# Three self-attention stages of a Perceiver kernel on one core: values spread by way of device memory, jobs in another order, cosines on GpSimd

## The chip, the core and the metric

One of the eight cores of a Trainium2 chip runs the whole program. The time is the device time of one execution in microseconds (us). The engines are TensorE (PE, with its weight loads as PEld), VectorE (DVE), ScalarE (ACT), GpSimd (POOL) and SyncE (SP), which here only issues DMAs. They run side by side and meet at semaphores; each takes its own instructions in order.

## The reference

A state x of 32 sequences with 32 tokens and 256 channels goes through twelve stages, each of which adds its result to x. Three of them are self-attentions with 16 heads of 16 channels over the 32 tokens of a sequence:

```python
# l0a: rotary q and k, a decay by distance for softmax, a gate
Q = _rotary(proj(Wq, bq)); K = _rotary(proj(Wk, bk)); V = proj(Wv, bv)
out = einsum('bhts,bhsd->bhtd', (Q @ K.T) / sqrt(16) * exp(-sigmoid(gamma) * clip(t - s, 0)), V)
x = x + silu(n @ Wg.T + bg) * out
# l1a: rotary, q and k divided by their norm, softmax, output weights
x = x + softmax(q @ k.T / sqrt(16)) @ v @ Wo + bo
# l3f: q divided by its norm, moved and scaled; softmax; 17 gate columns pick heads
h = softmax((q / norm(q) + e) * softplus(T) @ k.T / sqrt(16)) @ v
x = x + (h * gates(h)) @ Wp.T + bp
```

Here n is x after a layernorm without weights. All numbers are float32.

## The kernel before, in words

`self_attention` builds each of the three stages; `build` calls it as l0a, l1a and l3f. The 1024 tokens are cut into NG = 8 tiles of P = 128 rows, GB = 4 sequences of LQ = 32 tokens each. A tile g goes through jobs, for each of which TensorE fills one of two PSUM banks in turn, so that a job waits until the job two before it has been evacuated:

- `n` (line 1069): the normalised rows, made by VectorE, are transposed; ScalarE copies them to `nT` (1334).
- `qk` (1075): queries and keys from `nT`; ScalarE evacuates them to `qk` (1339, or four instructions with a bias, 1343).
- `v` (1078): values; VectorE (1198, with a bias row) or ScalarE (1347) evacuates them to `V_own`.
- `rot` (1084, l0a and l1a): a matrix that swaps the pairs; VectorE multiplies by the sine into `tmp` (1203), multiplies `qk` by the cosine (1204) and adds (1206).
- `gate` (1081, l0a): the gate; VectorE adds a bias (1230), ScalarE applies Silu (1403).
- `norm` (1087, l1a and l3f): VectorE squares into `tmp` (1212), TensorE sums within heads, ScalarE makes the reciprocal root by a logarithm (1351) and an exponential (1353) into `rstd`, and VectorE scales (1217 to 1220).

VectorE then spreads the queries over two masked heads (`two_heads`, 1224), and TensorE computes scores (1098). With softmax, VectorE takes the row maxima (1182) and subtracts them (1183), ScalarE exponentiates (1360), VectorE sums, divides and transposes to `pT` (1187 to 1192). In l0a VectorE multiplies by the decay (1175) and transposes (1180). TensorE multiplies by the values (1113). For this it needs each sequence's values on each of four groups of 32 partitions: SP copies them from `V_own` into `V` by 16 DMAs of 32 x 256 a tile (1317), each counted on a semaphore. In l1a and l3f ScalarE copies the heads (1366), TensorE transposes them (1120), ScalarE copies that (1374), and TensorE multiplies by the output weights (1126; in l3f also by 17 gate columns, 1129). VectorE adds the result to x (1246). In l3f ScalarE keeps it first (1379), and VectorE weighs four tiles at once, after tiles 3 and 7 (`gate_heads`, 1247 to 1274).

The order of all this is written out by hand, as one loop on each engine with a software pipeline: in step `it` TensorE projects tile `it`, takes scores of tile `it - 1` and weighted values and output of tile `it - 2`. An instruction waits behind all that stand ahead of it on its engine, needed or not. GpSimd only raises the variances to the power -1/2 (`power`, 188 and 193).

## Time and profile before

| | us |
|---|---|
| median of 3 runs | 4350.17 (4343.62 to 4352.81) |
| the profiled execution | 4349.88 |
| its span | 4348.1 |
| TensorE busy in the span | 3857.8 (89%) |
| VectorE busy | 2601.9 (60%) |
| ScalarE busy | 1840.4 (42%) |
| GpSimd busy | 309.6 (7%) |

The shares are means over twelve stages with different limits, so they do not tell what bounds the three stages here; the views by stretch and by time do. A row of the timeline gives the start, the length, the engine, the line, the operation, what it writes and reads, the shape and the count. In brackets stands how long the engine was idle before it, and what ended that.

### The profile page before, as it was taken

To read this page: it belongs to the slowest core of one execution; us is meant where nothing else is said; L and a number is where in the kernel's file an instruction comes from. 1 tells how busy PE (TensorE), PEld (TensorE's weight loads), DVE (VectorE), ACT (ScalarE), POOL (GpSimd) and SP (SyncE) were. 2 spreads that over 40 slices of the span, in tenths; PEclk is the share of its full clock that TensorE was granted. 3 is DMA by queue.
4 is the path that set the end of the run, shared out by engine and by line. 5 is a ranking of instruction groups with operands and counts; after the bars stand their busy time and mean duration, and the time that the engine had idled before them with its cause. 6 is when DMAs were issued, how large, how long until landed. Compare 5 with 4: busy or idle time off the path is not lost. (4 is left out here: it accounts for less than half of the span.)

```text
span 4348.1 us, 100504 instructions
## 1 busy us (share of the span) xinstructions
PE 3857.8 (89%) x41564; PEld 2896.4 (67%) x41564; DVE 2601.9 (60%) x5431; ACT 1840.4 (42%) x5087; POOL 309.6 (7%) x560
## 2 busy tenths in 40 slices
PE   7986995999999999999999998659678879888866
PEld 6765984677777777777777776548545569555535
DVE  3435113777777777777777775641157757446635
ACT  2221321444555455455445444212166736346522
POOL 0000101000000000000000000020111100000000
PEclk9997997999999999999999999969899979999977
DMA  4111484001101101101111100127654410000001
GB/s 155 61 63 41 150 298 166 31 31 53 50 31 53 50 31 53 50 31 53 50 33 50 50 31 11 48 83 288 215 166 147 154 47 1 26 30 30 11 2 49
DMA packets 135347, 323.03 MB, mean 74 GB/s; under 512 B 35496, under 2 KB 94056, under 8 KB 110448
## 3 DMA queue, kind: packets, MB, share of 16 engines
q1 hardware_dynamic: 131824, 308.22, 21.2%
q0 software_dynamic: 3072, 8.39, 0.5%
q8 instruction: 333, 5.46, 0.5%
q14 instruction: 118, 0.97, 0.1%
HBM read 289.01 MB, written 14.94 MB: 70 GB/s over the span
## 5 line engine op out<-in xcount | busy, mean ns | idle before, releaser
L2580 ACT COPY layers_pT<-banks 128x512 f32<-128x512 f32 x384 | 227.7, 593 | 551.3 <-PE banks L2348 550.6
L2272 PE MATMUL banks<-ctx_tiles,weights_a 128*128 128x512 f32 x768 | 363.7, 596 | 0.0
L2279 PE MATMUL banks<-weights_a,ctx_tiles 128*128 128x256 f32 x1536 | 363.1, 379 | 0.0
L2573 ACT ACTIVATE layers_probs<-banks,layers_negmax 128x256 f32<-128x256 f32 x768 | 354.9, 481 | 13.7 <-DVE layers_negmax L2438 6.8
L2279 PEld LDWEIGHTS banks<-weights_a,ctx_tiles 128*128 128x128 f32 x1536 | 284.7, 190 | 76.1 <-issue 46.4
L2416 DVE TENSOR_TENSOR layers_V<-banks,rows_a 128x512 f32<-128x512 f32 x192 | 132.8, 692 | 220.5 <-PE banks L2279 216.6
L2348 PE MATMUL banks<-const,layers_probs 128*128 128x128 f32 x1536 | 244.0, 281 | 2.8 <-ACT layers_pT L2580 2.8
L2348 PEld LDWEIGHTS banks<-const,layers_probs 128*128 128x128 f32 x1536 | 171.1, 141 | 106.2 <-issue 96.2
L2437 DVE TENSOR_REDUCE layers_negmax<-banks 128x4 f32<-128x1024 f32 x192 | 233.8, 1218 | 3.0 <-PE banks L2340 2.8
L2540 ACT ACTIVATE layers_KT<-banks,layers_less_last 128x256 f32<-128x256 f32 x384 | 162.4, 481 | 157.5 <-PE banks L2272 157.5
L2340 PE MATMUL banks<-layers_KT,layers_qblk 32*64 32x256 f32 x3072 | 210.6, 388 | 0.0
L2272 PEld LDWEIGHTS banks<-ctx_tiles,weights_a 128*128 128x128 f32 x768 | 132.0, 192 | 93.2 <-issue 93.2
L2323 PE MATMUL banks<-layers_dm_nT,weights_b 128*128 128x128 f32 x1536 | 189.7, 277 | 0.6 <-ACT layers_dm_nT L2535 0.6
L2323 PEld LDWEIGHTS banks<-layers_dm_nT,weights_b 128*128 128x128 f32 x1536 | 181.6, 194 | 0.9 <-ACT layers_dm_nT L2535 0.9
L2328 PE MATMUL banks<-weights_b,layers_hid 128*128 128x256 f32 x768 | 176.9, 383 | 4.2 <-ACT layers_hid L2563 3.1
L2328 PEld LDWEIGHTS banks<-weights_b,layers_hid 128*128 128x128 f32 x768 | 142.4, 190 | 37.3 <-issue 18.6
L2573 ACT ACTIVATION_READ_ACCUMULATOR layers_probs<-banks,layers_negmax 128x1 f32 x768 | 162.7, 212 | 0.0
L2340 PEld LDWEIGHTS banks<-layers_KT,layers_qblk 32*64 32x64 f32 x3072 | 98.2, 131 | 73.4 <-issue 40.3
L2563 ACT ACTIVATE layers_hid<-banks,layers_dm_cols 128x128 f32<-128x128 f32 x384 | 111.1, 383 | 62.0 <-PE banks L2323 61.9
L2360 PE MATMUL banks<-layers_pT,layers_V 128*32 128x64 f32 x6144 | 125.5, 221 | 6.0 <-ACT layers_pT L2580 6.0
L2861 PE MATMUL banks<-weights_a,ctx_tiles 128*128 128x512 f32 x256 | 129.8, 636 | 1.0 <-DVE l2x_own L2936 0.5
L2360 PEld LDWEIGHTS banks<-layers_pT,layers_V 128*32 128x32 f32 x6144 | 96.2, 110 | 46.7 <-issue 40.0
(715 smaller groups left out, 8188.4 us busy)
## 6 DMA issues: line engine op xcount, KB each, us to landing
ctx_tiles<-in_ctx SPq DMA_DIRECT2D x65, 1028.0 KB, 5.1
weights_a<-in_L_w SPq DMA_DIRECT2D x44, 1024.0 KB, 5.3
l2x_B<-positions SPq DMA_DIRECT2D x32, 1280.0 KB, 5.9
weights_b<-in_L_w SPq DMA_DIRECT2D x32, 1024.0 KB, 5.2
weights_c<-in_L_w SPq DMA_DIRECT2D x16, 1024.0 KB, 7.2
weights_b<-in_L_xattn_w SPq DMA_DIRECT2D x12, 1024.0 KB, 7.4
l0x_key_rows<-in_ctx_rows SPq DMA_DIRECT2D x32, 256.0 KB, 2.7
ctx_tiles<-in_ctx_keys SPq DMA_DIRECT2D x32, 256.0 KB, 2.8
```

The costliest lines, as they stand in the source:

```text
L2272: last = mm(o.rearrange("p (j k) -> p j k", j=2), ca_wk[:, c, m * P:(m + 1) * P], keys, start=c == 0, stop=c == DC - 1)
L2279: last = mm(o[:, b * D:(b + 1) * D], E.ctx[:, tile % 2, c, first:first + P], ca_wv[:, c], start=c == 0, stop=c == DC - 1)
L2323: last = mm(o[:, i * P:(i + 1) * P], dm_w1[:, c, m * P:(m + 1) * P], dm_nT[:, c], start=c == 0, stop=c == DC - 1)
L2328: last = mm(o[:, 0:D], hid[:, m], dm_w2[:, m], start=m == 0, stop=m == FC - 1)
L2340: last = mm(ps[half, r // 2, a * KW:(a + 1) * KW], qblk[rows, tile % 2, cc, j + a], KT[rows, tile % 2, cc, (j + a) * KW:(j + a + 1) * KW], ...
L2348: last = tr(ps[:, TURN, (KC * t + c) * P:(KC * t + c + 1) * P], probs[:, cc, j, t, c * P:(c + 1) * P], E.c("ident"))
L2360: last = mm(ps[32 * i:32 * (i + 1), PV, j * 64:(j + 1) * 64], V[:, pos % 2, KC * j + c, cc * P + 32 * i:cc * P + 32 * (i + 1)], pT[:, k % ...
L2416: last = v.tensor_tensor(V[:, tile % 2, KC * arg:KC * (arg + 1)], o.rearrange("p (b d) -> p b d", b=KC), E.rA[:, 0].unsqueeze(1).to_broadc ...
L2437: link(v.tensor_reduce(peak, ps[:, 0:2].rearrange("p t (a x) -> p t a x", a=2), AX.X, ALU.max, negate=True))
L2540: last = a(KT[:, pos % 2, m, j * KW:(j + 1) * KW], o[:, j % 2 * KW:(j % 2 + 1) * KW], ACT.Identity, bias=less_last[:, pos // NG % 2, m, se ...
L2573: a(probs[:, cc, i, t], ps[:, t, i % 2 * KW:(i % 2 + 1) * KW], ACT.Exp, bias=negmax[:, cc, t, i:i + 1], accum_out=totals[:, cc, t, i:i + 1 ...
L2580: nc.scalar.copy(pT[:, k % 4].rearrange("p t c x -> p (t c x)"), ps[:, TURN]).then_inc(s["copied"], 1)
```

## The change

Four things, all in `self_attention`:

1. SP stores a tile's `V_own` to device memory (`value_rows`) with one DMA, waits until it has landed, and loads it into `V` by four DMAs, one for each group of 32 partitions. `V_own` is free again when the store has landed.
2. The loops of TensorE, VectorE and ScalarE are written in another order, and `n` stands second in the list of jobs.
3. With rotation, GpSimd multiplies `qk` by the cosine into a tile of its own, `turned_qk`, and VectorE only adds.
4. In l1a VectorE scales the keys alone, and scales and masks the queries in the same two instructions.

```diff
                  "rot": "dve", "gate": "dve", "norm": "act"}
-    kinds = ["qk", "v"] + (["rot"] if rope else []) + (["gate"] if gated else []) + ["n"] + (["norm"] if norms else [])
+    kinds = ["qk", "n", "v"] + (["rot"] if rope else []) + (["gate"] if gated else []) + (["norm"] if norms else [])
     jobs = [("n", 0)]
...
         s, handles = signals(st, nc, tag, "n_ready job_done evac_dve evac_act rotated squared logs rstd_ready qblk_ready scores_done shifted exp_done pT_ready "
-                             "pv_done attn_ready turned attnT_ready y_ready y_taken gate_in gate_ready scored gate_exp v_spread0 v_spread1 dve_step var_ready added_eps power_ready")
+                             "pv_done attn_ready cosine_ready turned attnT_ready y_ready y_taken gate_in gate_ready scored gate_exp v_stored v_spread0 v_spread1 dve_step var_ready added_eps power_ready")
 
...
         tmp, rstd = sb("tmp", [4 * P]), sb("rstd", [4 * P])
+        turned_qk = sb("turned_qk", [4 * P]) if rope else None
         V_own = sb("V_own", [2, D])
...
         def wait_spread(eng, tile):
-            eng.wait_ge(s[f"v_spread{tile % 2}"], 16 * GB * 4 * (tile // 2 + 1))
+            eng.wait_ge(s[f"v_spread{tile % 2}"], 16 * 4 * (tile // 2 + 1))
 
...
                         job("qk", it)
-                    if tile_in(it - 1):
-                        scores(it - 1)
+                    if tile_in(it + 1):
+                        job("n", it + 1)
                     if tile_in(it):
...
                             job("rot", it)
+                    if tile_in(it - 1):
+                        scores(it - 1)
                     if tile_in(it - 2):
...
                         job("gate", it)
+                    if tile_in(it) and norms:
+                        job("norm", it)
                     if tile_in(it - 2) and not gated:
                         turned(it - 2)
-                    if tile_in(it + 1):
-                        job("n", it + 1)
-                    if tile_in(it) and norms:
-                        job("norm", it)
                     if tile_in(it - 2) and not gated:
...
                     if g >= 2:
-                        wait_spread(dve, g - 2)
+                        dve.wait_ge(s["v_stored"], 16 * (g - 1))
                     v.tensor_tensor(V_own[:, g % 2], bank(number["v", g])[:, 0:D], bv_row, ALU.add).then_inc(s["evac_dve"], 1)
...
                     wait_job(dve, "rot", g)
-                    q4, t4 = qk[:, g % 2].rearrange("p a (j q) -> p (a j) q", j=GB), tmp.rearrange("p (a q) -> p a q", q=LQ)
+                    q4 = qk[:, g % 2].rearrange("p a b -> p (a b)")
+                    t4 = tmp.rearrange("p (a q) -> p a q", q=LQ)
                     v.tensor_tensor(t4, bank(number["rot", g]).rearrange("p (a q) -> p a q", q=LQ), E.c("sin").unsqueeze(1).to_broadcast([P, 16, LQ]), ALU.mult).then_inc(s["evac_dve"], 1)
-                    link(v.tensor_tensor(q4, q4, E.c("cos").unsqueeze(1).to_broadcast([P, 16, LQ]), ALU.mult))
                     wait_evacuated(dve, "rot", g)
-                    link(v.tensor_tensor(q4, q4, t4, ALU.add))
+                    dve.wait_ge(s["cosine_ready"], g + 1)
+                    v.tensor_tensor(q4, turned_qk[:], tmp[:], ALU.add).then_inc(s["rotated"], 1)
+                    dve.wait_ge(s["rotated"], g + 1)
 
...
                     dve.wait_ge(s["rstd_ready"], g + 1)
+                    if unit_norm:
+                        own = qk[:, g % 2, 2:4].rearrange("p a b -> p (a b)")
+                        v.tensor_tensor(own, own, rstd[:, 2 * P:4 * P], ALU.mult)
+                        for h in range(2):
+                            last = v.scalar_tensor_tensor(qblk[:, g % 2].rearrange("p m j (h q) -> p m j h q", h=2)[:, :, :, h],
+                                                          qk[:, g % 2, 0:2].rearrange("p m (j q) -> p m j q", j=GB), E.c("qmask32")[:, h:h + 1],
+                                                          rstd[:, 0:2 * P].rearrange("p (m j q) -> p m j q", m=DC, j=GB), ALU.mult, ALU.mult)
+                        last.then_inc(s["qblk_ready"], 1)
+                        return
                     link(v.tensor_tensor(q2, q2, rstd[:, 0:norm_cols], ALU.mult))
...
                 for it in range(NG + 3):
-                    if tile_in(it - 1):
-                        shift(it - 1)
                     if tile_in(it - 3) and not gated and heads_gate is None:
...
                         square(it)
+                    if tile_in(it - 1):
+                        shift(it - 1)
                     if tile_in(it) and gated:
...
                             scale(it)
-                        two_heads(it)
+                        if not unit_norm:
+                            two_heads(it)
 
...
                     wait_evacuated(sp, "v", g)
+                    sp.dma_start(E.value_rows[g], V_own[:, g % 2]).then_inc(s["v_stored"], 16)
+                    sp.wait_ge(s["v_stored"], 16 * (g + 1))
                     if g >= 3:
                         sp.wait_ge(s["pv_done"], g - 2)
-                    for j in range(GB):
-                        for b in range(4):
-                            sp.dma_start(V[LQ * b:LQ * (b + 1), g % 3, j], V_own[LQ * j:LQ * (j + 1), g % 2]).then_inc(s[f"v_spread{g % 2}"], 16)
+                    for b in range(4):
+                        sp.dma_start(V[LQ * b:LQ * (b + 1), g % 3], E.value_rows[g].rearrange("(j p) d -> p j d", j=GB)).then_inc(s[f"v_spread{g % 2}"], 16)
 
...
             def _(pool):
-                for g in range(NG):
-                    power(E, pool, s, g, stats[:, g, 8:9], stats[:, g, 7:8], 1e-5)
+                for g in range(NG + 3):
+                    if rope and g >= 3:
+                        wait_evacuated(pool, "qk", g - 3)
+                        if g >= 4:
+                            pool.wait_ge(s["rotated"], g - 3)
+                        nc.gpsimd.tensor_tensor(turned_qk.rearrange("p (a q) -> p a q", q=LQ), qk[:, (g - 3) % 2].rearrange("p a (j q) -> p (a j) q", j=GB),
+                                                E.c("cos").unsqueeze(1).to_broadcast([P, 16, LQ]), ALU.mult).then_inc(s["cosine_ready"], 1)
+                    if g < NG:
+                        power(E, pool, s, g, stats[:, g, 8:9], stats[:, g, 7:8], 1e-5)
 
...
                         if g >= 2:
-                            wait_spread(act, g - 2)
+                            act.wait_ge(s["v_stored"], 16 * (g - 1))
                         last = nc.scalar.copy(V_own[:, g % 2], o[:, 0:D])
...
                         keep_output(it - 3)
+                    if heads_gate is not None and it - 3 in (GB - 1, NG - 1):
+                        exponentiate_odds((it - 3) // GB)
+                    if tile_in(it + 1):
+                        take("n", it + 1)
+                    if tile_in(it):
+                        take("v", it)
                     if tile_in(it - 1) and decay is None:
                         exponentials(it - 1)
-                    if heads_gate is not None and it - 3 in (GB - 1, NG - 1):
-                        exponentiate_odds((it - 3) // GB)
-                    if tile_in(it):
-                        take("v", it)
                     if tile_in(it - 2) and not gated:
...
                         a(gate[:, it % 3], gate[:, it % 3], ACT.Silu).then_inc(s["gate_ready"], 1)
+                    if tile_in(it) and norms:
+                        take("norm", it)
                     if tile_in(it - 2) and not gated:
                         turned(it - 2)
-                    if tile_in(it + 1):
-                        take("n", it + 1)
-                    if tile_in(it) and norms:
-                        take("norm", it)
 
...
         E.sorted_out = nc.dram_tensor("sorted_out", (NBLK, P, D), F32).ap()
+        E.value_rows = nc.dram_tensor("value_rows", (NG, P, D), F32).ap()
         E.positions = nc.dram_tensor("positions", (2, NG, GB, 16 * NK * LQ), F32).ap()
```

What order this gives in the middle of l1a. `l1a_qk` are rotated queries and keys, `weights_a` and `rows_a` weights and bias rows, `const` holds tables and small matrices, `banks` is PSUM. Line numbers grow by up to 21 with the change.

TensorE, one tile, before:

```order
L1075 MATMUL banks<-l1a_nT,weights_a 128x128 x8
L1098 MATMUL banks<-l1a_qk,l1a_qblk 64x32 x32
L1078 MATMUL banks<-weights_a,l1a_nT 128x256 x2
L1084 MATMUL banks<-l1a_qk,const 128x512
L1113 MATMUL banks<-l1a_V,l1a_pT 32x16 x64
L1120 MATMUL banks<-const,l1a_attn 128x128 x2
L1069 MATMUL banks<-const,l1a_n 128x128 x2
L1087 MATMUL banks<-l1a_tmp,const 128x512
L1126 MATMUL banks<-weights_a,l1a_attnT 128x256 x2
```
and with the change:

```order
L1076 MATMUL banks<-l1a_nT,weights_a 128x128 x8
L1070 MATMUL banks<-const,l1a_n 128x128 x2
L1079 MATMUL banks<-weights_a,l1a_nT 128x256 x2
L1085 MATMUL banks<-l1a_qk,const 128x512
L1099 MATMUL banks<-l1a_qk,l1a_qblk 64x32 x32
L1114 MATMUL banks<-l1a_V,l1a_pT 32x16 x64
L1088 MATMUL banks<-l1a_tmp,const 128x512
L1121 MATMUL banks<-const,l1a_attn 128x128 x2
L1127 MATMUL banks<-weights_a,l1a_attnT 128x256 x2
```

The scores of the tile before (64x32) moved from second place to behind the rotation, the transposes of the next tile (`l1a_n`) from behind the turned heads to second place, the norm (`l1a_tmp`) ahead of them.

ScalarE, one tile, before:

```order
L1339 COPY l1a_qk<-banks 128x512
L1360 ACTIVATE l1a_probs<-l1a_probs 128x512
L1347 COPY l1a_V_own<-banks 128x256
L1366 COPY l1a_attn<-banks 128x4x4x16
L1374 COPY l1a_attnT<-banks 128x128 x2
L1334 COPY l1a_nT<-banks 128x256
L1351 ACTIVATE l1a_rstd<-banks,const 128x512
L1353 ACTIVATE l1a_rstd<-l1a_rstd 128x512
```
and with the change:

```order
L1360 COPY l1a_qk<-banks 128x512
L1355 COPY l1a_nT<-banks 128x256
L1368 COPY l1a_V_own<-banks 128x256
L1381 ACTIVATE l1a_probs<-l1a_probs 128x512
L1387 COPY l1a_attn<-banks 128x4x4x16
L1372 ACTIVATE l1a_rstd<-banks,const 128x512
L1374 ACTIVATE l1a_rstd<-l1a_rstd 128x512
L1395 COPY l1a_attnT<-banks 128x128 x2
```

The exponentials (`l1a_probs`) moved behind the two evacuations, the norm (`l1a_rstd`) ahead of the copy of the turned heads (`l1a_attnT`), which is last now.

VectorE, from the row maxima to the sum of the exponentials, before:

```order
L1182 TENSOR_REDUCE l1a_max<-banks 128x16
L1183 TENSOR_TENSOR l1a_probs<-banks,l1a_max 128x512
L1244 TENSOR_TENSOR l1a_attn<-banks,rows_a 128x256
L1246 TENSOR_TENSOR x_state<-x_state,l1a_attn 128x256
L1203 TENSOR_TENSOR l1a_tmp<-banks,const 128x512
L1204 TENSOR_TENSOR l1a_qk<-l1a_qk,const 128x512
L1206 TENSOR_TENSOR l1a_qk<-l1a_qk,l1a_tmp 128x512
L1212 TENSOR_TENSOR l1a_tmp<-l1a_qk 128x512
L1187 TENSOR_REDUCE l1a_sum<-l1a_probs 128x16
```
and with the change, from the stage's result:

```order
L1256 TENSOR_TENSOR l1a_attn<-banks,rows_a 128x256
L1258 TENSOR_TENSOR x_state<-x_state,l1a_attn 128x256
L1205 TENSOR_TENSOR l1a_tmp<-banks,const 128x512
L1208 TENSOR_TENSOR l1a_qk<-l1a_turned_qk,l1a_tmp 128x512
L1215 TENSOR_TENSOR l1a_tmp<-l1a_qk 128x512
L1183 TENSOR_REDUCE l1a_max<-banks 128x16
L1184 TENSOR_TENSOR l1a_probs<-banks,l1a_max 128x512
L1188 TENSOR_REDUCE l1a_sum<-l1a_probs 128x16
```

The maxima and the subtraction moved from ahead of the result, rotation and squares to behind them, and the multiplication of `l1a_qk` by the cosine (from `const`) is gone.

## Rows read from the trace of the kernel before

**Rows 1.** Busy time by stretch, l0a, l1a, l3f: us, PE, PEld, DVE, ACT, POOL, PEclk, DMA, GB/s.
```profile
318.00:422.00 104.00, 70.59 (x1760) 56.42 (x1760) 52.76 (x120) 15.96 (x49) 6.88 (x16) 0.80 0.19 51
2729.00:2838.00 109.00, 79.20 (x1792) 58.83 (x1792) 74.65 (x144) 32.81 (x73) 8.31 (x16) 0.88 0.19 49
4225.00:4342.00 117.00, 82.84 (x1808) 70.38 (x1808) 68.17 (x174) 37.71 (x107) 6.66 (x16) 0.72 0.16 38
```

**Rows 2.** Timeline of SP's DMA queue, l0a.
```profile
326.95 90.59 SPq L1317 DMA_DIRECT2D l0a_V<-l0a_V_own  x128
```

**Rows 3.** Busy time in one tile of l0a at full clock.
```profile
371.88:380.67 8.79, 7.62 (x220) 6.18 (x221) 6.50 (x16) 1.82 (x6) 0.90 (x2) 1.00 0.21 51
```

**Rows 4.** Timeline of TensorE, l0a: first and last projections, last weighted values.
```profile
321.90 3.69 PE L1075 MATMUL banks<-l0a_nT,weights_c 128*128 128x128 f32 x16 [0.46 <-ACT l0a_nT L1334]
...
389.65 2.02 PE L1075 MATMUL banks<-l0a_nT,weights_c 128*128 128x128 f32 x16 [1.17 <-ACT l0a_nT L1334]
...
418.92 1.57 PE L1113 MATMUL banks<-l0a_V,l0a_pT 32*32 32x16 f32 x128 [9.10 <-DMA l0a_V<-l0a_V_own]
```

**Rows 5.** Timeline of VectorE, the last sum of l0a.
```profile
421.41 0.42 DVE L1239 TENSOR_TENSOR x_state<-x_state,l0a_attn 128x256 f32<-128x256 f32 x1
```

**Rows 6.** Timeline of TensorE, l1a.
```profile
2732.32 3.40 PE L1075 MATMUL banks<-l1a_nT,weights_a 128*128 128x128 f32 x16 [0.46 <-ACT l1a_nT L1334]
...
2775.22 1.95 PE L1075 MATMUL banks<-l1a_nT,weights_a 128*128 128x128 f32 x16
...
2779.93 1.02 PE L1084 MATMUL banks<-l1a_qk,const 128*128 128x512 f32 x2
...
2785.17 1.03 PE L1126 MATMUL banks<-weights_a,l1a_attnT 128*128 128x256 f32 x4
...
2786.03 1.95 PE L1075 MATMUL banks<-l1a_nT,weights_a 128*128 128x128 f32 x16
...
2810.53 1.95 PE L1075 MATMUL banks<-l1a_nT,weights_a 128*128 128x128 f32 x16
```

**Rows 7.** Timeline of VectorE, l1a, in the same tile.
```profile
2779.11 0.69 DVE L1182 TENSOR_REDUCE l1a_max<-banks 128x16 f32<-128x512 f32 x1 [1.26 <-PE banks L1098]
...
2779.83 0.69 DVE L1183 TENSOR_TENSOR l1a_probs<-banks,l1a_max 128x512 f32<-128x512 f32 x1
...
2781.95 0.68 DVE L1204 TENSOR_TENSOR l1a_qk<-l1a_qk,const 128x512 f32<-128x512 f32 x1
```

**Rows 8.** Timeline of ScalarE, l1a, in the same tile.
```profile
2777.21 0.59 ACT L1339 COPY l1a_qk<-banks 128x512 f32<-128x512 f32 x1 [1.30 <-PE banks L1075]
...
2780.56 0.63 ACT L1360 ACTIVATE l1a_probs<-l1a_probs 128x512 f32<-128x512 f32 x1 [2.77 <-DVE l1a_probs L1183]
...
2782.47 0.37 ACT L1366 COPY l1a_attn<-banks 128x256 f32<-128x256 f32 x1 [1.02 <-PE banks L1113]
...
2783.37 0.43 ACT L1374 COPY l1a_attnT<-banks 128x128 f32<-128x128 f32 x2 [0.53 <-PE banks L1120]
...
2785.37 0.69 ACT L1351 ACTIVATE l1a_rstd<-banks,const 128x512 f32<-128x512 f32 x1 [1.29 <-PE banks L1087]
...
2786.09 0.63 ACT L1353 ACTIVATE l1a_rstd<-l1a_rstd 128x512 f32<-128x512 f32 x1
```

**Rows 9.** Timeline of TensorE, l3f: first and last projections.
```profile
4228.55 3.79 PE L1075 MATMUL banks<-l3f_nT,weights_c 128*128 128x128 f32 x16 [0.46 <-ACT l3f_nT L1334]
...
4306.06 3.30 PE L1075 MATMUL banks<-l3f_nT,weights_c 128*128 128x128 f32 x16
```

**Rows 10.** Timeline of ScalarE, l3f: evacuation of the projections with a bias.
```profile
4278.48 1.14 ACT L1343 ACTIVATE l3f_qk<-banks,cols 128x128 f32<-128x128 f32 x4 [2.37 <-PE banks L1075]
```

**Rows 11.** Busy time in l3f's last gating of the heads.
```profile
4333.60:4341.90 8.30, 0.00 (x0) 0.00 (x0) 7.04 (x27) 0.32 (x2) 0.00 (x0) 0.50 0.00 0
```

**Rows 12.** DMA issues of the page: a store to device memory (KB each, us to landing).
```profile
sorted_out<-l0f_y SPq DMA_DIRECT2D x23, 128.0 KB, 2.7
```

**Rows 13.** GpSimd by line: ns of one (least/median/most), first and last start, forms.
```profile
L3035 POOL TENSOR_TENSOR ctx_tiles<-ctx_tiles x32: 1037/1044/2292, 3142.8 to 3446.7; 128x512 f32<-128x512 f32 x32
```

## The prediction

> **What bounds the kernel now.** The change touches three stages of the program, the self-attentions l0a, l1a and l3f, so I read the stretches first: they last 104, 109 and 117 us of a span of 4348.1 us, with a mean granted clock of 0.80, 0.88 and 0.72 [rows 1]. Everything outside them keeps its instructions and its time. Then the DMA queue's timeline: in l0a SP issues 128 copies in 90.59 us without a pause worth the name [rows 2], 16 a tile, so SP needs about 10 us for a tile's values. Then TensorE's timeline. In l0a an undisturbed tile has 7.62 us of TensorE work in a pitch of 8.79 us at full clock [rows 3], less than SP's 10: SP falls behind, and at the end the stage waits for it. The last tile's projections (line 1075) start at 389.65, but its probability-times-values product (line 1113) only at 418.92, after 9.10 us of waiting for the DMA into V [rows 4], and the stage's last sum starts at 421.41 [rows 5].
>
> l1a is bound elsewhere. A tile there takes 10.81 us from projections to projections [rows 6]; VectorE stands still only 1.26 us in that, before the row maxima, waiting for the scores [rows 7]. So VectorE is the bound, and SP's 10 us hide. l3f is mixed: 77.5 us for seven tiles (4228.55 to 4306.06 [rows 9]), one of which carries the gating of the heads, 8.3 us [rows 11].
>
> **The change, part by part.** *Spread of values.* Sixteen copies a tile become one store to device memory, a wait, and four loads. SP issued a copy every 0.7 us (90.59/128 [rows 2]). A 128 KB store to device memory lands in 2.7 us [rows 12]; I take that for the store and for each load too. So V is ready 0.6 + 2.7 + 4 x 0.6 + 2.7 = 8.4 us after its values are evacuated; SP is busy 6 us of that, less than any tile's pitch. Bounds: about 5 us if transfers land at once, 13 if they take twice as long. The values are used two tiles later, so only the last tile could show it.
>
> *l0a.* The new order on TensorE is projections, next tile's transposes, values, rotation, scores, weighted values, gate. ScalarE's evacuation of the projections, formerly covered by the scores, now stands open before the values job: 0.9 us of waiting, where before TensorE waited about 1.2 us for the evacuated transposes. The pitch stays about 8.7 (7.62 + 0.9 and hand-overs). Tile 0 has neither scores nor weighted values and tile 1 only scores: 7.9 and 7.3. Seven tiles: 7.9 + 7.3 + 5 x 8.7 = 58.7, and a slow patch of 1, against 67.8 (321.90 to 389.65 [rows 4]): 8 us gained. The tail: masked queries ready 10.8 us after the last projections start, scores 1.1, decay and transposition 1.5, weighted values 1.6, two sums 0.9, hand-overs and a slow clock 1.6: 17.5, against 32.2 (389.65 to 421.83 [rows 4, 5]): 14 us gained. V, evacuated 4.9 us after those projections start, is ready at 13.3; it is needed at 14. Together **-22 us** for l0a; the upper bound of the round trip gives back 4.
>
> *The cosine on GpSimd.* It takes 0.68 us off VectorE a tile [rows 7] and costs GpSimd 1.04 us alone, 2.29 at worst for the same shape [rows 13]. It starts when ScalarE has evacuated the projections and is wanted after rotation and sine, some 2.7 us later in l1a. So it is hidden at either price, and counts as nothing; without that cover it would cost the difference, under 0.5 us a tile.
>
> *l1a.* Here the order makes a loop out of nearly everything. The exponentials of the tile before stand behind the row maxima, which VectorE now takes only after sine, sum and squares of this tile; ScalarE's copy of the heads, its logarithm and exponential for the norm and its copy of the turned heads stand behind those exponentials; and TensorE's output product, last in its tile, waits for that copy. In start-to-start steps: projections to evacuation 1.99 [rows 6, 8], evacuation 0.65 with the hand-over [rows 8], values 0.86 (as long as the output job, of the same form), rotation 1.06 [rows 6], five VectorE steps, four of 0.72 and one of 0.69 with 0.04 of hand-over [rows 7], ScalarE 0.63 + 0.37 + 0.69 + 0.63 + 0.43 = 2.75 [rows 8], output 0.92 with its hand-over. Sum **11.8 us**, against 10.81: VectorE has less to do and waits more. The rewritten scaling (three instructions on 256 columns in place of three) lies in that wait: nothing. First tiles: tile 0, without a predecessor, 9.3; tile 1, without output, 7.9; tile 2, whose VectorE is still late from tile 1, 12.5; then 4 x 11.8. Sum 76.9, against 78.2 (2732.32 to 2810.53 [rows 6]). That 78.2 holds its slow patches; 76.9 holds none.
>
> *l3f.* The same loop without rotation, sine, sum and squares (-3.2), with scores in their place (+1.1), four biased evacuations of 1.14 in all [rows 10] for 0.59, a norm of half the columns, a biased copy and 17 gate columns: 10.5 us a tile. First tiles 6.6, 5.9, 13.0, then 3 x 10.5, and the tile with the gating 18: 75, against 77.5.
>
> *Slow clock.* Projections take 1.95 us at full clock and up to 3.79 at the lower of TensorE's two levels, 1.2 GHz for 2.4 [rows 6, 9]: 1.8 us for each patch that falls on them. Nothing before shows how often the new order meets one. Bounds: never, and always. Mean clocks of 0.88 and 0.72 [rows 1] say neither; I take four patches in each of the two stages, 7.2 us, since the loop leaves TensorE more waiting than VectorE's chain did. So l1a +6, l3f +5. Tails of both: the same links, nothing.
>
> **Sum.** 4349.9 (the profiled execution, 1.8 us more than its span, 0.3 under the median of the runs) - 22 + 6 + 5 = **4339 us**.
>
> A rule bears on that clock. The stage with the lowest clock, l3f, had TensorE busy 71% of its stretch, l0a with 0.80 had it busy 68% [rows 1]: busy share alone does not order them. The Trainium skill, "TensorE: Matmul & The Clock Gate", Part 1, says that the throttled state is the default and that activity releases it. Taken alone, the rule would turn every longer wait into slow clock and add up to the 44 us of rival C; these rows make it only likelier, so the sum keeps four patches.
>
> **The rivals.** *B, a patch in every tile:* seven a stage, 12.6 us each instead of 7.2: 4349, no change. For: the loop repeats the same pauses in each tile. Against: the tile of l1a in [rows 6] has pauses too, and its projections take 1.95, which is full clock.
>
> *C, slower:* in l1a and l3f TensorE drops to 1.2 GHz and stays there, because a slower loop waits longer still. The price for a tile is what the loop holds of TensorE: projections 1.84, values, rotation and output some 0.9 each in l1a: 4.6; in l3f 4.3. Over five tiles each, 44 us on the sum without patches (-26): 4368. The gain is gone once six in ten of those tiles are slow, and eight in ten make the kernel slower by more than a measurement can miss. For: 0.72 in l3f now. Against: 0.88 in l1a.
>
> *D, no patches:* -22 - 1.3 - 2.5: 4324.
>
> *E, the round trip does not do what it says:* loads out of device memory so late that l0a's tail stays: 4339 + 14 = 4353. Against: twice the landing time gives back only 4.
>
> *F, the two engines in each other's way:* the 2.29 us beside the usual 1.04 [rows 13] show GpSimd held up by something. If a cosine held VectorE up by its own 1.04 us in all 16 tiles, on the loop, that is 17 us: 4356. Against: VectorE waits for the rotation while the cosine runs. The Trainium skill, "SBUF — State Buffer", "Who interferes with whom", has VectorE instructions with two SBUF inputs and GpSimd reads excluding each other for a whole instruction. By that rule F needs two such instructions to meet, which here is mostly tile 2 of l1a.
>
> **How the numbers follow.** Chances: the forecast 0.42, B 0.26, C 0.12, D 0.12, E 0.05, F 0.03. What a measurement of this kernel can tell from no change is about 0.2%, 8.7 us, so faster means under 4341.5. The forecast's own spread of some 7 us lies two thirds below that, D wholly, B hardly: faster 0.47. B, the rest of the forecast and E make no change: 0.39. C and F with edges: slower 0.14. The range runs from just above D to past B, E and F, leaving out C and a part of D: 4326 to 4358.
>
> **What would show it.** l0a some 80 us long, TensorE never waiting for a DMA into V, SP idle between tiles. In l1a a pitch of 11.8 at full clock with VectorE waiting about 2 us for the rotation, and ScalarE's copy of the turned heads the last thing before output. In l3f a pitch of 10.5. The forecast is wrong if the pitch of l1a is under 10.8, if the clocks of l1a and l3f rise, or if V is still waited for.

## The result and the profile after

The changed kernel takes 4363.32 us (median of 22 runs, 4349.39 to 4372.5), the kernel before 4352.01 us (22 runs, 4338.39 to 4362.21): ratio 1.0025, 95% interval 1.0015 to 1.0035. It is slower, by a quarter of a per cent, where 4339 and a gain were forecast. 4363.32 lies above the forecast's range.

The three stages tell where the time went. The view of busy time by stretch, for each stage from its first projections to its last sum; the columns are those of [rows 1]. Before:

```profile
321.90:421.83 99.93, 69.90 (x1758) 56.13 (x1758) 50.50 (x114) 15.58 (x48) 5.30 (x12) 0.81 0.18 44
2732.32:2838.11 105.79, 78.51 (x1790) 58.55 (x1790) 72.51 (x138) 31.16 (x71) 6.73 (x12) 0.89 0.17 44
4228.55:4341.88 113.33, 82.15 (x1806) 70.09 (x1806) 65.91 (x168) 36.06 (x105) 5.05 (x12) 0.73 0.16 39
```

After:

```profile
328.00:410.93 82.93, 66.54 (x1758) 53.82 (x1758) 46.06 (x106) 15.60 (x48) 15.33 (x20) 0.87 0.22 66
2723.68:2842.33 118.65, 91.22 (x1790) 66.88 (x1790) 66.12 (x130) 29.85 (x71) 15.52 (x20) 0.77 0.16 47
4233.69:4364.63 130.94, 91.03 (x1806) 75.83 (x1806) 66.03 (x168) 35.77 (x105) 5.42 (x12) 0.68 0.14 42
```

l0a gained 17.0 us, l1a lost 12.9, l3f lost 17.6: together +13.5, beside a difference of the medians of 11.3. Look at two columns of l1a. VectorE has less work than before (66.12 for 72.51), as intended. TensorE does the same work (1790 records; a float32 product leaves two) and is busy 91.22 us for 78.51: the clock column explains that, 0.77 for 0.89. (The profiled execution was the slowest of the 22, 4372.5 us. l0a begins 6 us later in it than before, 328.00 for 321.90; the code ahead of it is the same, and with the experiments below l0a begins at 321.6 to 328.5. That part is not the change's.)

The tail of l0a, which [rows 4] showed waiting 9.10 us for the DMA into V, is gone. The view of line 1114 (weighted values, all three stages) lists what TensorE waited for ahead of it:

```profile
its engine sat idle before it (us, times) until:
  issue: 38.2, 32
  DVE l0a_pT L1181: 0.7, 1
  DVE l0a_attn L1248: 0.7, 1
  DVE l1a_attn L1256: 0.6, 1
  ACT l3f_y_all L1400: 0.6, 1
```

No DMA stands there. The 38.2 us are not all lost: the view counts products and weight loads apart, and these overlap. In TensorE's timeline the waits marked "issue", for which the profile shows no releaser, sum to 17.4 us in the three stages. SP's queue in the last tile of l0a, then the loads' line:

```profile
393.95 0.34 SPq L1326 DMA_DIRECT2D value_rows<-l0a_V_own  x1
395.67 2.47 SPq L1331 DMA_DIRECT2D l0a_V<-value_rows  x4
```

```profile
L1331 SPq DMA_DIRECT2D l0a_V<-value_rows x32: 303/432/1625, 335.7 to 397.7; - x32
...
DMA to landing us min/median/max: 2.1/2.7/3.9
```

The last load is issued at 397.7; loads land 2.1 to 3.9 us after their issue, so it has landed 5.9 to 7.7 us after the store was issued; 8.4 was forecast. GpSimd's cosines, against VectorE's 0.68 [rows 7]:

```profile
L1340 POOL TENSOR_TENSOR l0a_turned_qk<-l0a_qk,const x8: 1262/1266/1267, 332.4 to 393.9; 128x512 f32<-128x512 f32 x8
L1340 POOL TENSOR_TENSOR l1a_turned_qk<-l1a_qk,const x8: 1260/1267/1270, 2727.8 to 2817.2; 128x512 f32<-128x512 f32 x8
```

All sixteen take 1.26 to 1.27 us. Nine of them ran beside a VectorE instruction (each with one of its inputs in PSUM), seven beside none.

Now the loop of l1a. TensorE's timeline, from one tile's projections (line 1076) to the next:

```profile
2797.72 3.62 PE L1076 MATMUL banks<-l1a_nT,weights_a 128*128 128x128 f32 x16
...
2808.12 0.24 PE L1114 MATMUL banks<-l1a_V,l1a_pT 32*32 32x16 f32 x6 [1.92 <-issue]
2808.30 1.93 PE L1088 MATMUL banks<-l1a_tmp,const 128*128 128x512 f32 x2
...
2811.98 2.07 PE L1127 MATMUL banks<-weights_a,l1a_attnT 128*128 128x256 f32 x4 [1.33 <-ACT l1a_attnT L1395]
2813.85 2.65 PE L1076 MATMUL banks<-l1a_nT,weights_a 128*128 128x128 f32 x16
```

and ScalarE's in the same tile:

```profile
2801.37 0.59 ACT L1360 COPY l1a_qk<-banks 128x512 f32<-128x512 f32 x1 [5.58 <-PE banks L1076]
...
2807.61 0.63 ACT L1381 ACTIVATE l1a_probs<-l1a_probs 128x512 f32<-128x512 f32 x1 [4.06 <-DVE l1a_probs L1184]
...
2810.26 0.69 ACT L1372 ACTIVATE l1a_rstd<-banks,const 128x512 f32<-128x512 f32 x1 [1.47 <-PE banks L1088]
2810.98 0.63 ACT L1374 ACTIVATE l1a_rstd<-l1a_rstd 128x512 f32<-128x512 f32 x1
2811.51 0.41 ACT L1395 COPY l1a_attnT<-banks 128x128 f32<-128x128 f32 x2
```

The chain is the one forecast: ScalarE's copy of the turned heads comes last, and the output product (1127) waits for it, 1.33 us here. The tile takes 16.13 us where the walk gave 11.8. Projections to evacuation take 3.65 us for 1.99, exponentials to output 4.37 for 2.75, output to projections 1.87 for 0.92. The first and the last of these are TensorE's products at half their speed: the projections take 3.62 us, 1.95 at full clock [rows 6]. In the second, ScalarE waits 1.47 us for the norm's product (1088), which takes 1.93 us for 1.10 at full clock (in e3 below) and starts late, since it stands behind the weighted values. These held a wait that had no place in the prediction: 1.92 us "issue" in their middle, where the profile shows nothing that TensorE waits for.

Of the four loop tiles from 2756.10 to 2813.85 the first two take 13.1 us and hold no such pause; the last two take 15.5 and 16.1 and hold one of 1.59 and 1.92 us. The mean is 14.4. In l3f two tiles look like this:

```profile
4289.91 2.07 PE L1127 MATMUL banks<-weights_c,l3f_attnT 128*128 128x256 f32 x4 [0.90 <-ACT l3f_attnT L1395]
...
4292.49 3.76 PE L1076 MATMUL banks<-l3f_nT,weights_c 128*128 128x128 f32 x16
...
4304.18 2.08 PE L1127 MATMUL banks<-weights_c,l3f_attnT 128*128 128x256 f32 x4 [1.23 <-ACT l3f_attnT L1395]
...
4306.77 3.74 PE L1076 MATMUL banks<-l3f_nT,weights_c 128*128 128x128 f32 x16
```

Output and projections run at the lower level in these tiles. The three loop tiles take 15.64, 13.56 and 14.28 us; the middle one holds no pause.

### The profile page after: what moved, and what is told of

It reads as the page before. It is cut to its first block and busy times, and to the rows that moved or that the text cites. A ratio compares the mean times of both kernels' runs of the same rounds, so it can differ in the third digit from the quotient of the medians.

```text
span 4370.7 us, 100254 instructions
## 1 busy us (share of the span) xinstructions
PE 3887.4 (89%) x41564; PEld 2917.9 (67%) x41564; DVE 2588.1 (59%) x5415; ACT 1839.0 (42%) x5087; POOL 328.2 (8%) x576
```

## The experiments

The theory after the result: the new order makes the chain of l1a and l3f long, as walked; its waits bring TensorE's lower clock into every tile, and that, not the chain, is what was underpriced. Rivals: the chain is longer than walked, whatever the clock; or the spread, the cosine or the scaling does the harm. In the table the stages go from first projections to last sum, in us, with the mean granted clock. The ratio is to the kernel before on the same chip, whose medians there were 4353 to 4355 for the experiments.

| | l0a | l1a | l3f | median | ratio (95%) |
|---|---|---|---|---|---|
| before | 99.9 (0.81) | 105.8 (0.89) | 113.3 (0.73) | 4352.0 | |
| changed | 82.9 (0.87) | 118.7 (0.77) | 130.9 (0.68) | 4363.3 | 1.0025 (1.0015 to 1.0035) |
| e1 spread alone | 82.7 (0.89) | 105.9 (0.89) | 109.2 (0.75) | 4330.1 | 0.9939 (0.9924 to 0.9953) |
| e2 old order in l1a, l3f | 83.7 (0.87) | 98.1 (0.90) | 110.2 (0.73) | 4325.7 | 0.9931 (0.9918 to 0.9943) |
| e3 fill | 85.1 (0.84) | 105.7 (0.90) | 118.6 (0.79) | 4340.5 | 0.9968 (0.9956 to 0.9980) |
| e4 heads first | 86.1 (0.84) | 106.3 (0.84) | 123.4 (0.72) | 4346.3 | 0.9982 (0.9973 to 0.9992) |
| e5 scores back | 84.5 (0.82) | 122.0 (0.74) | 116.6 (0.70) | 4356.2 | 1.0008 (0.9999 to 1.0016) |
| e6 old order everywhere | 76.8 (0.92) | 97.5 (0.90) | 108.5 (0.75) | 4316.1 | 0.9917 (0.9902 to 0.9933) |
| e7 e6, cosine on VectorE | 82.9 (0.87) | 104.5 (0.88) | 110.2 (0.73) | 4326.0 | 0.9937 (0.9922 to 0.9951) |
| e8 e2 and fill | 78.7 (0.91) | 94.0 (0.92) | 109.7 (0.76) | 4315.6 | 0.9923 (0.9907 to 0.9938) |
| e9 e6 and fill | 76.7 (0.92) | 94.2 (0.92) | 109.2 (0.77) | 4313.7 | 0.9909 (0.9892 to 0.9927) |
| e10 e6, norm first | 76.1 (0.93) | 107.4 (0.87) | 121.5 (0.71) | 4339.1 | 0.9968 (0.9954 to 0.9982) |

Each stage time is that of one execution. How far such times go apart without a cause in the stage's own code can be read in l0a, where five kernels run the same code (changed, e2, e3, e4, e8): 78.7 to 86.1 us. With the old order and the cosine on GpSimd (e6, e9, e10) it is 76.1 to 76.8, and l3f, the same code in e1, e2, e6 and e7, takes 108.5 to 110.2.

**e1, the spread alone**, in the kernel before:

```diff
...
-                    for j in range(GB):
-                        for b in range(4):
-                            sp.dma_start(V[LQ * b:LQ * (b + 1), g % 3, j], V_own[LQ * j:LQ * (j + 1), g % 2]).then_inc(s[f"v_spread{g % 2}"], 16)
+                    sp.dma_start(E.value_rows[g], V_own[:, g % 2]).then_inc(s["v_stored"], 16)
+                    sp.wait_ge(s["v_stored"], 16 * (g + 1))
...
+                    for b in range(4):
+                        sp.dma_start(V[LQ * b:LQ * (b + 1), g % 3], E.value_rows[g].rearrange("(j p) d -> p j d", j=GB)).then_inc(s[f"v_spread{g % 2}"], 16)
...
```

> The kernel before, in its own order, with the values spread by way of device memory and nothing else. If the round trip does what it says, l0a loses its tail behind the copies: last projections to the stage's end 32.2 us before, some 20 after (-12), l1a loses its one wait of 2.3 us for a DMA, l3f nothing: about 4338 us against 4352, ratio 0.997. If the spread by itself costs l1a or l3f something (transfers in the way of other work), those two stages grow from 106 and 113 us towards the 119 and 131 of the changed kernel and the ratio goes to 1.003.

Measured: ratio 0.9939. l0a falls by 17.2 us, of which 15.7 are the tail (32.2 to 16.5); so it has the whole gain that the changed kernel has there. l1a stays: its one wait was an "issue" wait and no DMA (I had that wrong), and is still there with 2.77 us. l3f gains 4.2 us that I had not expected. The trace of before has a likely reason: SP's 128 copies for l3f take 91.35 us, 11.4 a tile, more than most of that stage's tiles, and TensorE waits once for the DMA into V (in e1 it doesn't):

```profile
4327.06 1.55 PE L1113 MATMUL banks<-l3f_V,l3f_pT 32*32 32x16 f32 x128 [0.69 <-DMA l3f_V<-l3f_V_own]
```

The spread does no harm anywhere.

**e2, the old order in the two stages with a norm**, `old = norms` choosing between the two orders on each engine; on TensorE:

```diff
...
+    old = norms
...
+                    if old and tile_in(it - 1):
+                        scores(it - 1)
-                    if tile_in(it + 1):
+                    if not old and tile_in(it + 1):
                         job("n", it + 1)
...
```

> The changed kernel with the old order of jobs, of all three engines, in the two stages that have a norm (l1a, l3f); spread, cosine on GpSimd and the shorter scaling stay, and l0a keeps the new order. If the order made l1a and l3f slower: l0a keeps its 17 us of gain, l1a, bound by VectorE, gets under its old pitch of 10.8 us (one instruction of 0.7 us less and shorter scaling: about 9.9), so -6 against the kernel before, l3f as before: about 4329 us, ratio 0.995. If spread, cosine or scaling made them slower, l1a stays near 119 us and l3f near 131 and the ratio stays near 1.0025.

Measured: ratio 0.9931. l1a and l3f lose 20.6 and 20.7 us against the changed kernel, with everything else of the change in place; l1a's tiles take 9.94 us, where 9.9 was expected. The order did the harm.

**e3, TensorE filled**, in the changed kernel:

```diff
+                def fill(it, times):
+                    if tile_in(it) and norms:
+                        n = number["norm", it] + 1
+                        pe.wait_ge(s[evacuated[n - RB][0]], evacuated[n - RB][1])
+                        for _ in range(times):
+                            mm(bank(n)[:, 0:D], E.c("ident"), wv[:, 0], start=True, stop=True)
+
                 def turned(g):
+                    fill(g + 2, 1)
                     pe.wait_ge(s["attn_ready"], g + 1)
...
                 def output(g):
+                    fill(g + 2, 2)
                     pe.wait_ge(s["attnT_ready"], g + 1)
```

> The changed kernel, where in l1a and l3f TensorE does matmuls without a purpose while it waits: one before the heads are transposed, two before the output product (0.5 us each at full clock, into the bank that the next projections overwrite). If the low clock that follows TensorE's waits is what lengthened the loops (14.4 us a tile in l1a and 14.8 in l3f, where the walk at full clock gave 11.8 and 10.5), the pitch falls to 12 to 12.5 and 11 to 12 and the mean clocks rise from 0.77 and 0.68 to over 0.85: 15 to 25 us less than the changed kernel, 4338 to 4348, ratio 0.997 to 0.999. If the loop is long by itself and the clock only follows, the pitches stay and the filling costs up to 1 us a tile: ratio 1.0025 to 1.005.

Measured: ratio 0.9968. Eighteen more products a stage, and l1a is 13.0 us shorter, l3f 12.4. The two stages by stretch:

```profile
2723.82:2829.47 105.65, 85.97 (x1826) 64.12 (x1826) 65.81 (x129) 30.00 (x71) 15.50 (x20) 0.90 0.18 53
4216.88:4335.45 118.57, 85.18 (x1842) 70.94 (x1842) 66.00 (x168) 35.83 (x105) 5.35 (x12) 0.79 0.16 46
```

TensorE does more in l1a and is busy less, 85.97 us for 91.22, since the clock is 0.90 for 0.77. One tile of it, on TensorE (line 1123 is the fill):

```profile
2755.32 1.95 PE L1076 MATMUL banks<-l1a_nT,weights_a 128*128 128x128 f32 x16
...
2764.76 1.03 PE L1123 MATMUL banks<-weights_a,const 128*128 128x256 f32 x4
2766.06 1.13 PE L1136 MATMUL banks<-weights_a,l1a_attnT 128*128 128x256 f32 x4 [0.27 <-ACT l1a_attnT L1404]
2767.03 1.95 PE L1076 MATMUL banks<-l1a_nT,weights_a 128*128 128x128 f32 x16
```

Here is the chain of the prediction at full clock, with the output still waiting for the same copy: 11.71 us, where 11.8 was walked. Two of the four loop tiles take that; the other two hold a pause ("issue") of 0.60 and 1.78 us and take 12.58 and 12.51. That settles it for l1a: the chain was sized rightly, and what lies above it in the changed kernel is the lower clock and the pauses (a tile with one is 0.8 to 0.9 us longer than one without here, and 2.4 to 3.0 there). In l3f the expectation missed: 11 to 12 us and a clock over 0.85 were expected, the pitches are 12.7 to 13.7 and the clock is 0.79. Pauses of 1.0 to 2.0 us "issue" remain in the three loop tiles, the fill itself runs at the lower level there, and no run shows that loop undisturbed; its 10.5 is neither shown nor refuted.

**e4, ScalarE's order alone**:

```diff
-                    if tile_in(it - 1) and decay is None:
-                        exponentials(it - 1)
                     if tile_in(it - 2) and not gated:
                         heads(it - 2)
+                    if tile_in(it - 1) and decay is None:
+                        exponentials(it - 1)
...
-                    if tile_in(it) and norms:
-                        take("norm", it)
                     if tile_in(it - 2) and not gated:
                         turned(it - 2)
+                    if tile_in(it) and norms:
+                        take("norm", it)
```

> The changed kernel with ScalarE's order alone altered: the copy of the heads ahead of the exponentials, and the copy of the turned heads ahead of the norm's logarithm and exponential, as in the kernel before. This takes about 1.5 us out of the chain to the output product in each tile (logarithm and exponential 1.3 us, exponentials 0.6 less what still waits). If the chain through ScalarE is the loop, l1a and l3f lose 1.5 us in each of about 5 tiles: 15 us less, ratio 0.999. If shorter waits also bring back the clock, another 10 to 20 us: ratio 0.995 to 0.997. If the low clock stays with these waits and ScalarE only waits elsewhere, no change: ratio 1.0025.

Measured: ratio 0.9982; l1a 12.3 us shorter, l3f 7.5. At full clock a tile of l1a now takes 10.19 us (2760.22 to 2770.41), 1.5 less than e3's 11.71, as expected:

```profile
2759.25 1.13 PE L1127 MATMUL banks<-weights_a,l1a_attnT 128*128 128x256 f32 x4 [0.52 <-ACT l1a_attnT L1395]
2760.22 1.95 PE L1076 MATMUL banks<-l1a_nT,weights_a 128*128 128x128 f32 x16
```

The wait before output went from 1.13 us or more to 0.52 to 0.90, and these tiles keep full clock; the later ones, at 12.3 and 14.8, have pauses of 1.6 and 2.2 us "issue" and don't. l3f's output still waits 0.7 us, and its clock, 0.72, is still low.

In three tiles of l1a in this run GpSimd's cosine meets VectorE's sum into x, whose two inputs both lie in SBUF. GpSimd and VectorE in the first of them:

```profile
2752.85 1.26 POOL L1340 TENSOR_TENSOR l1a_turned_qk<-l1a_qk,const 128x512 f32<-128x512 f32 x1
```

```profile
2753.21 1.18 DVE L1258 TENSOR_TENSOR x_state<-x_state,l1a_attn 128x256 f32<-128x256 f32 x1
```

The sum takes 1.18 us each time, and 0.42 in the other five tiles and in all eight of the changed kernel, where none meets a cosine.

**e5, the scores back** behind the projections, on TensorE alone:

```diff
                         job("qk", it)
+                    if tile_in(it - 1):
+                        scores(it - 1)
                     if tile_in(it + 1):
                         job("n", it + 1)
...
                             job("rot", it)
-                    if tile_in(it - 1):
-                        scores(it - 1)
```

> The changed kernel with TensorE's scores alone moved back to where they stood, right behind the projections; the other engines and the rest of TensorE keep the new order. In the changed kernel TensorE stands in the middle of the weighted values for want of instructions, 5.7 us in l0a, 4.9 in l1a, 6.8 in l3f together, against 1.9, 2.8 and 0.9 with the spread alone in the old order. If this comes of scores and weighted values (64 and 128 short instructions) standing next to each other, the pauses fall to 1 to 3 us a stage and the two waits for the evacuated projections go: 8 to 15 us less than the changed kernel, ratio 0.999 to 1.0005. If the pauses come of the transfers or of where the program's code lies, they stay and so does the time: ratio 1.0015 to 1.0035.

Measured: ratio 1.0008, just outside what was expected. The pauses behaved: TensorE's "issue" waits, nearly all in the weighted values, sum to 0.3, 1.3 and 0.9 us in the three stages, for 5.7, 4.9 and 6.8. l3f is 14.3 us shorter. The pauses there are gone, and the scores now fill the wait for its evacuated projections; which of the two counts for more is not separated. The wait ahead of l3f's output is still there, and in two of its loop tiles full clock follows it:

```profile
4276.13 1.13 PE L1127 MATMUL banks<-weights_c,l3f_attnT 128*128 128x256 f32 x4 [1.23 <-ACT l3f_attnT L1395]
...
4277.46 2.03 PE L1076 MATMUL banks<-l3f_nT,weights_c 128*128 128x128 f32 x16
```

After the same wait of 1.23 us the changed kernel has 2.08 and 3.74 (4304.18, above). So this wait by itself does not bring the lower clock.

l0a and l1a are not shorter. In l0a TensorE now waits in each tile, 0.7 to 2.7 us, for VectorE's masked queries, in l1a in most tiles, 1.1 us or more, for VectorE's squares ahead of the norm's product. Products behind these waits run at the lower level. In l0a:

```profile
363.91 1.13 PE L1099 MATMUL banks<-l0a_qk,l0a_qblk 32*64 32x32 f32 x64 [1.66 <-DVE l0a_qblk L1236]
...
366.67 1.91 PE L1085 MATMUL banks<-l0a_qk,const 128*128 128x512 f32 x2
```

(1.02 us at full clock [rows 6].) In l1a:

```profile
2778.59 1.88 PE L1088 MATMUL banks<-l1a_tmp,const 128*128 128x512 f32 x2 [1.21 <-DVE l1a_tmp L1215]
```

Half a return to the old order removes one wait and makes another.

**e6, the old order everywhere** (`old = True`; spread, cosine and scaling stay).

> The changed kernel with the old order of jobs in all three stages; spread, cosine on GpSimd and shorter scaling stay. If the whole gain of l0a is the spread's, l0a lasts 82 to 84 us as with the spread alone (82.7) and with the new order (82.9): ratio 0.993, as with the old order in l1a and l3f alone. If the new order is worth the 8 us in l0a that the prediction gave it, l0a grows to 90: ratio 0.995.

Measured: ratio 0.9917. Neither reading held for l0a. It is 76.8 us, 6 shorter than with the new order (82.9) or with the spread alone (82.7): the new order costs there too, by 2 to 9 us over all kernels that have it. l0a by stretch, of e1 and of e6:

```profile
328.21:410.93 82.72, 66.10 (x1758) 53.95 (x1758) 50.24 (x114) 15.58 (x48) 5.29 (x12) 0.89 0.23 66
```

```profile
328.13:404.96 76.83, 63.73 (x1758) 51.61 (x1758) 45.37 (x105) 15.59 (x48) 15.48 (x20) 0.92 0.25 71
```

**e7, as e6 with the cosine back on VectorE.**

```diff
...
+                    link(v.tensor_tensor(q4, q4, E.c("cos").unsqueeze(1).to_broadcast([P, 16, LQ]), ALU.mult))
                     wait_evacuated(dve, "rot", g)
-                    dve.wait_ge(s["cosine_ready"], g + 1)
-                    v.tensor_tensor(q4, turned_qk[:], tmp[:], ALU.add).then_inc(s["rotated"], 1)
-                    dve.wait_ge(s["rotated"], g + 1)
+                    link(v.tensor_tensor(q4, q4, t4, ALU.add))
...
```

> The same (old order everywhere, spread, shorter scaling) with the cosine back on VectorE. l1a lasted 105.9 us with the spread alone and 98.1 with spread, cosine on GpSimd and shorter scaling. If VectorE bounds it, the cosine is 0.72 us of that in each tile: l1a 103 to 104 us, l0a and l3f unchanged, ratio 0.9945. If GpSimd's multiplication holds VectorE up, taking it away costs less: l1a 98 to 101.

Measured: ratio 0.9937; l1a 104.5, so the cosine is worth 7.0 us there, in line with 8 tiles at 0.72, and the shorter scaling 1.4 (e1 to e7). I had not expected the 6.1 in l0a: nearly all of it lies in its second and third tiles (9.93 and 11.83 us, 7.77 and 8.64 with GpSimd); the tiles behind them take 8.64 to 8.66 in e7, 8.64 to 8.99 in e6. In these two tiles e7's projections take 3.09 and 2.81 us, 2.02 in e6: much of the 6.1 is the lower clock at the stage's start, and not VectorE's time. It is no accident of one execution, since e1, with the cosine on VectorE too, has 82.7; how the cosine brings it about is not shown.

**e8 and e9, fill in the old order**, one product ahead of the transposed heads in l1a and l3f; e8 with the new order in l0a, e9 with the old one everywhere. The diff is e9's; e8 leaves out `and norms`, which is the same, since l0a has no such job. Five tiles of a stage get the product.

```diff
                 def turned(g):
+                    if tile_in(g + 3) and norms:
+                        n = number["n", g + 3]
+                        pe.wait_ge(s[evacuated[n - RB][0]], evacuated[n - RB][1])
+                        mm(bank(n)[:, 0:D], E.c("ident"), wv[:, 0], start=True, stop=True)
                     pe.wait_ge(s["attn_ready"], g + 1)
```

> The kernel with the old order in l1a and l3f (new in l0a, all else of the change), and in each tile of l1a and l3f one matmul without a purpose (0.5 us) while TensorE waits for the copied heads. If the low clock of l3f (0.73) comes from that wait of 0.5 to 1.0 us and those about it, l3f falls from 110 to 103 to 106 us and l1a by 0 to 2: ratio 0.991 to 0.992. If other pauses (pipeline start, gating, end) hold the clock down there, no change: 0.993.

> Old order in all three stages with spread, cosine on GpSimd and shorter scaling, and in each tile of l1a and l3f one matmul without a purpose (0.5 us) ahead of the transposed heads, where TensorE waits 0.5 to 1 us. If that wait is what lowers the clock in l3f (0.75), l3f falls from 108.5 to 103 to 106 us: ratio 0.990 to 0.991. With the fill and the new order in l0a, l3f kept its 110 us and l1a lost 3.5, with pauses for want of instructions in other places; if it is those that count, no change to 0.9917 within 0.001.

Measured: 0.9923 and 0.9909. l3f missed both times: 109.7 and 109.2, no gain, though "issue" pauses there grew to 4.7 and 4.3 us. l1a gained 4.1 and 3.4, where its long pause of 2.2 to 2.5 us fell to 0.3. So one more product a tile moved the pauses about; whether a stage meets one depends on more than the order of its jobs. (e8 is 5 us shorter than e2 in l0a as well, where the two have the same code.) e9 has the lowest median, 4313.7; it cannot be told from e6.

**e10, one swap in e6**: ScalarE's norm ahead of the copy of the turned heads, as in the changed kernel. The diff is against e6.

```diff
-                    if old and tile_in(it - 2) and not gated:
-                        turned(it - 2)
                     if old and tile_in(it + 1):
                         take("n", it + 1)
                     if tile_in(it) and norms:
                         take("norm", it)
-                    if not old and tile_in(it - 2) and not gated:
+                    if tile_in(it - 2) and not gated:
                         turned(it - 2)
```

> Old order in all three stages with spread, cosine on GpSimd and shorter scaling, but on ScalarE the logarithm and exponential of the norm stand ahead of the copy of the turned heads, as in the changed kernel: one swap that puts a wait of some 2 us before TensorE's output product, where it had none. If the wait alone counts, l1a and l3f gain 2 us in about five tiles each: l1a 97.5 to 107, l3f 108.5 to 116, ratio 0.996. If such a wait also brings the low clock for the products behind it, as I take it to have done in the changed kernel, another 1.5 to 3 us a tile: l1a 113 to 122, l3f 120 to 130, ratio 0.999 to 1.002, and mean clocks under 0.80. If other work takes its place in the wait, no change: 0.992.

Measured: ratio 0.9968, +23 us on e6 by the medians. TensorE in l1a:

```profile
2745.87 1.13 PE L1128 MATMUL banks<-weights_a,l1a_attnT 128*128 128x256 f32 x4 [1.76 <-ACT l1a_attnT L1404]
2746.84 1.95 PE L1077 MATMUL banks<-l1a_nT,weights_a 128*128 128x128 f32 x16
...
2757.30 2.08 PE L1128 MATMUL banks<-weights_a,l1a_attnT 128*128 128x256 f32 x4 [1.76 <-ACT l1a_attnT L1404]
2759.17 2.60 PE L1077 MATMUL banks<-l1a_nT,weights_a 128*128 128x128 f32 x16
```

The same wait of 1.76 us before output, where e6 has none; after the first the products run at full clock, after the second at the lower level. l1a grows by 9.9 us, its middle tiles by 2.0 to 2.7 each, little more than the wait (a pause of 2.2 us that e6 had is gone too); l3f grows by 13.0, its loop tiles by 1.9 to 3.2 each for waits of 1.53 us, with its clock at 0.71 for 0.75. So the theory that each such wait brings the low clock missed in l1a. In l3f the length, 121.5, lies in the range given for it, but all its loop tiles except one grew by less than 1.5 us beyond the wait, and e5 has such waits with full clock behind them.

## Why the prediction was wrong

**The step that failed is "Slow clock".** I took four patches of 1.8 us in each of l1a and l3f, 14 us in all, and gave rival C, a clock that stays low, a chance of 0.12. l1a's loop tiles carry 14.4 - 11.7 = 2.7 us each, more than rival B's 1.8 and less than rival C's 4.6; l3f's three between 4263.29 and 4306.77 take 14.5 on average, 4.0 over the walk. What I held against C, the 0.88 of l1a before, was the clock of another loop, in which output did not wait. A loop that ends on a copy by ScalarE makes TensorE wait in each tile, and a patch that can fall on projections, norm and output together is not priced by the projections alone.

The prediction also put at nothing the "issue" pauses, for which it had no term: 4.9 us in l1a and 6.8 in l3f. With them the loop tiles fall into two kinds. Without a pause a tile is 1.4 us over the chain in l1a and 3.1 over the walk in l3f; with one it is 3.7 and 4.4 in l1a, 5.1 and 3.8 in l3f. e3, which takes most of the lower clock away, makes l1a 13.0 us shorter; e5, which takes most pauses away, makes l3f 14.3 us shorter with its clock hardly changed (0.70 for 0.68), but alters the order too. So in l1a the clock is shown to be the larger part. In l3f, where more than half of the miss lies (17.6 us lost for 5 forecast; l1a 12.9 for 6, l0a 17.0 gained for 22), clock and pauses are not separated.

That the time came out 5 us from rival C's 4368 is partly chance. Over the loops without patches l1a and l3f grew by 34 us together, where C has 44, and l0a gave back 5 that C does not hold. None of the prediction's three signs of being wrong appeared, for all three lay on the side of a better result: the pitch of l1a rose, the clocks fell, and V was not waited for.

**l1a, the chain: right.** 11.8 against 11.71 [e3], with the link that I named as last; of the first tiles the one is right, 9.34 for 9.3, the two behind it came out too short in the forecast, 9.19 for 7.9 and 13.89 for 12.5.

**l0a: -22 forecast, -17.0 measured, for another reason.** I gave 8 us to the new order and 14 to the tail. In the changed kernel the tiles gained 5 and the tail 12. The spread alone gives 17.2, the order takes back 6.1 (e6 against the changed kernel), the cosine gives 6.1 (e6 against e7). The order's debit goes with pauses and clock again: 5.7 us of "issue" and 0.87, for 0.5 and 0.92 in the old order.

**The spread: right in l0a.** No DMA is waited for; rival E is dead. SP's time for a tile before was 11.3 us (90.59/8 [rows 2]) and not about 10, and l3f gained 4.2 us by the spread, where the prediction had nothing. **The cosine: "nothing" was not tested in the changed order,** where VectorE waits in each tile anyway; in the old order it is worth 13 us over l0a and l1a. Rival F did not come about in the changed kernel: every cosine took 1.26 to 1.27 us and VectorE's rotation steps stayed at 0.69, since nothing with two SBUF inputs met a cosine. In e4 three such pairs met, and VectorE's sum took 1.18 us for 0.42. The Trainium skill's rule on two SBUF inputs ("SBUF — State Buffer", "Who interferes with whom") agrees with that.

By part, from the runs, l0a, l1a and l3f together: spread -21, shorter scaling and cosine -15 (e1 to e6), order +50 (e6 to the changed kernel). The ratios of the whole kernel give -27, -10 and +47. It is a good change undone by one part of it.

On the clock, e3 agrees with the Trainium skill, "TensorE: Matmul & The Clock Gate", Part 1, that activity releases the throttle: products without a purpose raised it from 0.77 to 0.90 and shortened the stage. The first of e10's waits and those of e5's l3f, with full clock behind them, show that one wait is not yet a lower clock; a price per wait cannot be read from these runs.

## What to carry to other kernels

Before an order is changed, follow the loop that it makes through all engines, and look where TensorE waits in it: each such place can cost the wait and then, though not every time, twice the time for the products behind it. Put what TensorE waits for first on the engine that makes it, and measure the parts of a change apart; here one of four cost more than the other three gained. Where a wait must stay, a few products without a purpose can be cheaper than the wait with its slow products, as in e3. And let some sign of being wrong lie on the side of a worse result.

## What was not expected

TensorE stands still for 0.2 to 2.8 us in the middle of the weighted values (64 short products, 128 records a tile), waiting for nothing that the profile shows. With the 32 short products of the scores directly ahead of them, in the changed kernel, "issue" waits sum to 17.4 us over the three stages; with the scores elsewhere (e5) to 2.5. The pauses have fixed places. In the five kernels with the old order in l1a and neither fill nor e10's swap (before, e1, e2, e6, e7) that stage has one pause, of 2.2 to 2.8 us, each time in its seventh tile ahead of the last four records of the weighted values. This speaks for the place in the program as the cause, and not for chance. From 2803 to 2809, around the pause that ends at 2808.12, the DMA view shows one transfer of instructions beside the spread's:

```profile
q8 instruction: 1, 0.02, 1.0%
```

That alone says little: in the whole of l1a this queue makes 14 such transfers in the changed kernel, with its three pauses, and 14 in e6, with its one.

The Trainium skill, "Runtime: NRT & Kernel Launch", "Instruction fetch mechanics", says that fetching the next block of instructions is mostly hidden. If these pauses are that fetch, it is not hidden in these places; that they are is likely and not shown.
